# Window attention: the normalisation of a row tile on VectorE, from a tensor_scalar to a three-operand operation

## What is computed

```python
def _layernorm(x, axis=-1, eps=1e-05):
    m = jnp.mean(x, axis=axis, keepdims=True)
    v = jnp.var(x, axis=axis, keepdims=True)
    return (x - m) / jnp.sqrt(v + eps)
...
x = x + _L0_xattn_ref(_layernorm(x, axis=-1), ctx_4096, ...)   # 8 heads, window 16
x = x + _L0_ffn_ref(_layernorm(x, axis=-1), ...)               # gated FFN
x = x + _L1_xattn_ref(_layernorm(x, axis=-1), ctx_4096, ...)   # cross attention, 32 heads
x = x + _L1_ffn_ref(_layernorm(x, axis=-1), ...)               # 8 experts, top 2
return x
```

## Time and profile before

| | us |
|---|---|
| median of 3 runs | 1135.47 |
| lowest, highest | 1133.59, 1136.64 |
| profiled execution, its time | 1131.74 |
| its span (first to last instruction) | 1129.9 |
| PE busy | 1043.6 (92%) |
| DVE busy | 660.0 (58%) |
| POOL busy | 515.3 (46%) |
| ACT busy | 352.3 (31%) |

### The profile page before, as it was taken

How to read it: one execution, slowest core, us unless ns; L and a number is a source line. 1 busy time by engine, 2 the same in 40 slices (tenths; PEclk the granted TensorE clock), 3 DMA queues, 4 the chain that set the end, 5 groups by cost and what they waited for, 6 DMA issues and landing times. The chain is left out here.

```text
span 1129.9 us, 24015 instructions
## 1 busy us (share of the span) xinstructions
PE 1043.6 (92%) x9170; PEld 867.2 (77%) x9170; DVE 660.0 (58%) x1357; ACT 352.3 (31%) x826; POOL 515.3 (46%) x594
## 2 busy tenths in 40 slices
PE   7899988999999879999999999999999999755993
PEld 3677777888887678888888888888888888534783
DVE  4799874544544675656565556656555565850424
ACT  3677744222222232222222222222222321211331
POOL 3555531422223355445454554444554542337755
PEclk9799999999999889999999999999999999986997
DMA  7100006656350021111011111111011100036768
GB/s 236 24 4 4 4 3 177 207 196 224 139 207 28 29 66 38 47 29 48 29 29 48 32 41 41 29 48 29 28 48 34 33 10 1 1 122 210 250 217 269
DMA packets 51806, 92.07 MB, mean 81 GB/s; under 512 B 10748, under 2 KB 24316, under 8 KB 51260
## 3 DMA queue, kind: packets, MB, share of 16 engines
q1 hardware_dynamic: 42108, 69.13, 19.2%
q10 hardware_dynamic: 6624, 12.06, 3.1%
q0 software_dynamic: 2976, 9.44, 2.5%
HBM read 77.25 MB, written 36.18 MB: 100 GB/s over the span
## 5 line engine op out<-in xcount | busy, mean ns | idle before, releaser
L121 PE MATMUL PS<-NTh,W 128*128 128x256 f32 (+2 forms) x688 | 216.5, 315 | 0.0
L122 PE MATMUL PS<-NTl,W 128*128 128x256 f32 (+2 forms) x688 | 214.0, 311 | 0.0
L123 PE MATMUL PS<-NTh,W 128*128 128x256 f32 (+2 forms) x688 | 213.9, 311 | 0.0
L122 PEld LDWEIGHTS PS<-NTl,W 128*128 128x128 f32 (+1 forms) x688 | 131.2, 191 | 6.9
L123 PEld LDWEIGHTS PS<-NTh,W 128*128 128x128 f32 (+1 forms) x688 | 129.4, 188 | 8.4
L121 PEld LDWEIGHTS PS<-NTh,W 128*128 128x128 f32 (+1 forms) x688 | 129.7, 189 | 7.1
L1501 POOL TENSOR_TENSOR W<-ca_raw,W 128x512 fp32r<-128x512 f32 x64 | 82.6, 1292 | 112.2 <-ACT W L1354 112.2
L1439 DVE TENSOR_REDUCE ca_su<-room 128x4 f32<-128x256 f32 x64 | 26.8, 419 | 154.5 <-ACT room L1368 154.5
L1468 DVE TENSOR_TENSOR room<-PS,ca_sinT 64x512 f32<-64x512 f32 (+1 forms) x192 | 115.0, 599 | 2.6
L121 PE MATMUL PS<-W,ca_aTh 128*128 128x512 f32 x256 | 106.9, 418 | 3.2 <-DVE X L1456 3.1
L122 PE MATMUL PS<-W,ca_aTh 128*128 128x512 f32 x256 | 101.3, 396 | 0.0
(11 more groups left out here) (253 smaller groups left out, 2350.3 us busy)
## 6 DMA issues: line engine op xcount, KB each, us to landing
ca_raw<-in_L_Wq SPq DMA_DIRECT2D x32, 256.0 KB, 2.8
ca_raw<-in_L_Wo SPq DMA_DIRECT2D x32, 256.0 KB, 2.6
rf_raw<-in_experts SPq DMA_DIRECT2D x28, 256.0 KB, 4.3
room<-slots ACTq DMA_DIRECT2D x23, 256.0 KB, 3.4
outs<-room ACTq DMA_DIRECT2D x23, 256.0 KB, 3.7
outs<-blank SPq DMA_DIRECT2D x11, 512.0 KB, 9.1
room<-in_L_Wg SPq DMA_DIRECT2D x10, 256.0 KB, 2.8
room<-in_L_Wu SPq DMA_DIRECT2D x10, 256.0 KB, 3.0
```

Of the source, the lines that this page charges most:

```text
L121: nc.tensor.matmul(out, l_hi, r_hi, start=first, stop=False)
L122: nc.tensor.matmul(out, l_hi, r_lo, start=False, stop=False)
L123: return nc.tensor.matmul(out, l_lo, r_hi, start=False, stop=last)
```

## The change

The normalisations of this stage, the eight at L528 and the seven at L222, are no longer a tensor_scalar with two values per partition (mean, inverse deviation) but a scalar_tensor_tensor: the mean stays a value per partition, and the inverse deviation is a second tensor operand, one element per partition repeated 512 times. The result is the same expression. The normalisations of the later stages stay.

```diff
+    def normalise_beside_gpsimd(self, vec, t, slot):
+
+        vec.wait_ge(self.rooted, t + 1)
+        self.nc.vector.scalar_tensor_tensor(self.row(t, slot), self.sh.X[:, t, :], self.mv[:, slot, 0:1],
+                                            self.rstd[:, slot:slot + 1].broadcast_to([P, E]), ALU.subtract, ALU.mult
+                                            ).then_inc(self.normed, 1)
...
                 def normalise(t, slot):
                     if not isinstance(t, int) or t >= 2:
                         vec.wait_ge(S["q_mm"], t - 1)
-                    one = bass.ds(t, 1)
-                    nc.vector.tensor_scalar(xn[:, slot:slot + 1, :], sh.X[:, one, :], mv[:, one, 0], rstd[:, one],
-                                            ALU.subtract, ALU.mult).then_inc(S["normed"], 1)
+                    nc.vector.scalar_tensor_tensor(xn[:, slot, :], sh.X[:, t, :], mv[:, t, 0:1], rstd[:, t:t + 1].broadcast_to([P, E]),
+                                                   ALU.subtract, ALU.mult).then_inc(S["normed"], 1)
...
                     if q == 2 and live(t - 2, TT - 1):
-                        norm.normalise(vec, t - 2, slot)
+                        norm.normalise_beside_gpsimd(vec, t - 2, slot)
```

## The result

Over 20 interleaved runs of each kernel the changed one takes 1137.67 us (1133.33 to 1140.61) and the one before 1134.59 us (1129.63 to 1138.13): a ratio of 1.003, 95% interval 1.0017 to 1.0043, which is 1.9 to 4.9 us slower. The prediction added 2.1 us (to 1137.6, from the 1135.47 of the three runs then known); over 20 runs the kernel before lies 0.9 us lower and the growth is 3.1 us, so that the two totals agree to 0.1 us is in part luck. The profiled execution of the changed kernel took 1136.59 us.

What follows compares the result with a forecast made beforehand. The prediction took VectorE and TensorE to be at a tie in the first stage's tiles and TensorE to bound the rest. 0.20 + 0.25 + 1.64 = +2.1 us on 1135.47 gave 1137.6 us, 8-in-10 range 1134.0 to 1140.8.

Steps and rivals of the forecast that it cites:

- Held up like the old form: At L528 and L222, the new form waits out GpSimd operations as the old does; blocked ones last about 1.48 us.
- the other order: At 33.88 us, GpSimd's copy L654 behind L528 may itself be held by VectorE; cost 0.
- +0.20 free, +0.25 held: Added time per changed normalisation: 0.20 us where GpSimd does not hold it up, 0.25 where it does.
- the upper end of the prediction (+0.28): Held normalisations: second input halves the rate, fixed part passes during the wait, 0.56 instead of 0.28 us after release.
- 0.41 us a tile: Four tiles from 61 to 130 us, one L222 and one L528 each: 0.41 us each, 1.64 together.
- The spare of 0.09: At L587 in each tile: 0.04 us to spare plus 0.05 from an earlier successor start, taken off the added 0.50.
- A tie, so that less VectorE work earns nothing: At L587 in the tiles, VectorE and TensorE tie: less VectorE work earns nothing, more costs nearly all of itself.
- The start, +0.45: L528 at the stage's start: first at 13.02 us costs 0.20 us, the one at 33.88 us 0.25, both delaying L404.
- The lone operations and the rest of the stage, 0: L528 at 48.58 us and L222 at 130.11, 146.65 and 165.78: covered by L587's waits for TensorE, 0.
- The clock rival: Low clock stretch from 27 to 41 us gets 5 us longer: 4.6 us in all, 1140.1 us; chance 0.16.
- the sum: Whole first stage: 0.20 + 0.25 + 1.64 = +2.1 us, with ends 1.6 and 2.4.

Runs made afterwards that it cites:

- the pair with the operand in PSUM and in SBUF: Changed form for tiles 3 to 7's query normalisation at its old place, inverse deviation copied to PSUM, read from PSUM or SBUF: 1132.48 and 1132.85 against 1134.65 us.
- the halves: Kernel before with the new form at only L528 or only L222: both 17.44 us a tile against 17.26; totals 1133.63 and 1134.98 against 1134.9 us.
- the old form behind the sums: Kernel before with its two-value normalisations issued after L566, when GpSimd's subtraction is nearly over: 17.26 us a tile, 1135.01 against 1134.9 us.
- the first kernel with the operand in PSUM: New-form query normalisation of tiles 3 to 7 just ahead of the score transpose, inverse deviation copied to PSUM and read there: 1139.20 us, one run.
- the low part early: L245's subtraction moved ahead of the score transpose: kernel before 1131.77 against 1134.77 us; changed kernel 1132.17 against 1134.65 us, 17.16 us a tile.

## Why the prediction was right, point by point

- **Held up like the old form**: shown by each of the 11 held operations (1.50 us; 1.48 had been predicted), and the reason by the pair with the operand in PSUM and in SBUF. At the start the other order is seen too, as the prediction had guessed: GpSimd's copy (L654, now L660) starts while the normalisation is at work and ends 0.14 us behind it in the kernel before and 0.13 in the changed one, where it takes 0.74 us instead of 0.47.
- **+0.20 free, +0.25 held**: measured +0.20 (0.743 to 0.746 against 0.541 to 0.547) and +0.27 (1.499 against 1.234). Behind the release 0.28 us are left of the old form's 0.54 and 0.54 to 0.55 of the new one's 0.75, while operations of 8 elements end 0.01 to 0.02 us behind it: what is left goes with the elements, and the part that doesn't passes during the wait, as the upper end of the prediction (+0.28) had it. The estimate from the Trainium skill's cycle formula (VectorE: DVE Perf Modes, "The TRN2 errata") had 0.33 and 0.59 us for the free forms, which is 0.21 and 0.15 us short of the measured; its difference, 0.27, is nearer to the held pair's than to the free pair's. The Trainium skill's rule on two SBUF inputs (SBUF — State Buffer, "Who interferes with whom") agrees with the pair, held from SBUF and not from PSUM. That whoever starts first holds the other off agrees with the tiles, where GpSimd starts 0.1 us ahead; in L1936's row the starts are 0.01 us apart and say nothing of the order.
- **0.41 us a tile**: measured 0.45. With 0.27 for the operation the term is 2 x 0.27 - 0.09 = 0.45. The spare of 0.09 is borne out by the halves, 0.18 each.
- **A tie, so that less VectorE work earns nothing**: the old form behind the sums, 1.2 us lighter a tile, 17.26 us. This is what would have gone wrong with a reading by busy share alone.
- **The start, +0.45**: L411 came 0.90 us after the first normalisation's start instead of 0.69, and 1.34 us after the third's instead of 1.08, as predicted (+0.21 and +0.26). But from the first normalisation to the first one for the next stage (near 61 us) the time grew by 0.22 us only, because the low stretch of the clock ended sooner after L411: L500 took 0.94 us where L493 had taken 1.10. So half of this term doesn't show. By how much it is wrong stays open, since the same stretch takes 47.8 to 48.2 us in three kernels that have the old form at the start, this one's 48.3 being little above them.
- **The lone operations and the rest of the stage, 0**: the whole stage, first to last bias addition, grew from 129.6 to 131.5 us, of which the four tiles are 1.8. The lone operations after 130 us were not quite covered: the tile behind each grew by 0.09 and 0.08 us, and VectorE's wait shrank by 0.18 and 0.17 us instead of 0.25. The hand-over L605 to L451 takes the rest: at 136.06 us L605 ends and L451 starts 0.15 us later. The prediction had looked at L587 alone.
- **The clock rival**: it did not decide. The stretch of low clock at the start did not get longer: on average from 27 to 41 us the clock was 0.56 and 0.63 in the two profiles of the changed kernel, against 0.52.

From the first normalisation to the last bias addition the changed kernel takes 163.0 us in both profiles and the kernel before 160.8: 2.2 us, where the sum had 2.1. In part the terms make up for each other, the start being smaller by 0.2 and the tiles and the rest larger by 0.2 each. This is 2.2 us of the 3.1 between the medians; the other 0.9 lies within the interval (1.9 to 4.9), and the comparison at an equal mean clock points to the clock of the executions for it. The profiles have the FFN 0.8 to 1.2 us longer in the changed kernel at the same mean clock of 0.90 in its first part, but the first kernel with the operand in PSUM also had 168.2 us at 0.90. Whether some of this belongs to the change, by where the end of the stage falls in the clock's stretch, is open.

## What to carry to other kernels

A VectorE operation with two tensor operands in SBUF waited here for a GpSimd operation that reads SBUF, just as the tensor_scalar did. To escape, put one operand in PSUM (0.75 us instead of 1.31) or the operation where GpSimd is nearly through (0.64 instead of 1.23), rather than give up the faster form. Before you price a longer or shorter instruction, look at who releases its successor: at a tie between two engines, time added is paid and time saved is not, and the costs of two parts don't simply add up. The gain lay in the hand-over that followed (L245 to L404), which the profile called "issue".

## What the runs showed that I had not expected

- Part of a held VectorE operation passes during the wait, in both forms: the two-value form, 0.54 us when free, needs 0.28 us after the release, and the three-operand form 0.54 instead of 0.75.
- Moving one operation of 0.68 us across two others made the stage 3.0 us shorter, though the held operations lasted 1.23 us as before.
- Spare time has to be counted at each hand-over. With the low part early VectorE idled for 0.55 us a tile, and 0.53 us of extra work still cost 0.32, all of it at L605's hand-over to L451.
